# Expert layers of a one-core MoE kernel with weight chunks as the stationary operand, and scatter-adds ordered by expert

## What is computed

```
x = x + attention(layernorm(x))
t = rows of x                                  # 2048 tokens of 256
n = layernorm(t)
p = softmax(n @ router_w + router_b)           # 8 experts
top_v, top_i = top_k(p, 2); top_v /= sum(top_v)
for each expert e:
    h = silu(n @ gate_w[e] + gate_b[e]) * (n @ up_w[e] + up_b[e])     # 256 -> 512
    y[e] = h @ down_w[e] + down_b[e]                                  # 512 -> 256
t = t + sum of top_v * y[e] over the two chosen experts
```

## Time and profile before

| | |
|---|---|
| median of 3 runs | 454.25 us |
| all runs | 455.29, 454.06, 454.25 us |
| span of the profiled execution (first to last instruction) | 453.7 us |
| own time of the profiled execution | not given beside the span |
| busy, share of the span | PE 76%, DVE 76%, POOL 64%, ACT 46% |
| mean granted TensorE clock | 0.851 |

### The profile page before, as it was taken

How to read it: one execution, slowest core, us unless ns; L and a number is a source line. 1 busy time by engine, 2 the same in 40 slices (tenths; PEclk the granted TensorE clock), 3 DMA queues, 4 the chain that set the end, 5 groups by cost and what they waited for, 6 DMA issues and landing times.

```text
span 453.7 us, 13159 instructions
## 1 busy us (share of the span) xinstructions
PE 346.5 (76%) x4491; PEld 214.4 (47%) x4492; DVE 343.3 (76%) x693; ACT 209.2 (46%) x343; POOL 288.8 (64%) x459
## 2 busy tenths in 40 slices
PE   0078677767866766697259998999999999999971
PEld 0077434444444454542023654656566566565540
DVE  6988799799899999877882776666776776677650
ACT  1047637755956857645501433334434434433430
POOL 5616456666666666644585367777877878788651
PEclk9997568668668668689569999999999999999995
DMA  8410002322322222507764132333233333323322
GB/s 197 123 36 1 2 2 96 95 94 97 95 92 92 92 95 94 144 2 194 219 248 139 25 48 46 48 56 58 46 56 55 51 49 55 58 46 58 56 25 23
DMA packets 24960, 35.27 MB, mean 78 GB/s; under 512 B 4992, under 2 KB 18304, under 8 KB 24160
## 3 DMA queue, kind: packets, MB, share of 16 engines
q1 hardware_dynamic: 16256, 24.46, 17.5%
q0 software_dynamic: 7488, 10.23, 14.1%
q10 hardware_dynamic: 1184, 0.14, 0.2%
HBM read 25.39 MB, written 9.44 MB: 77 GB/s over the span
## 4 chain that ended last, share of the span: by engine, by line
PE 25%; DVE 23%; issue 19%; POOL 13%; DMA 9%; ACT 5%; DVEq 2%; POOLq 1%; SPq 1%; ACTq 0%
PE bank L881 6%; DMA w_stage<-token_rows,q_hi 5%; POOL w_stage L513 4%; PE bank L902 3%; POOL small L509 3%; DVE att L1348 2%; PE bank L549 2%; DVE s_exp L1314 2%; DVE v_exp L1367 2%; PE bank L777 2%; DVE q_exp L1382 2%; POOL v_exp L488 2%; PE bank L664 2%; DVE maxes L1307 2%; DMA token_rows<-z_stack 1%
## 5 line engine op out<-in xcount | busy, mean ns | idle before, releaser
L881 PE MATMUL bank<-w_exp,w_stage 128*128 x468 | 113.7, 380 | 1.3 <-issue 0.2
L526 POOL DMA_INDIRECT out_dram<-w_stage,q_hi x39 | 62.4, 1600 | 16.9 <-issue 16.9
L881 PEld LDWEIGHTS bank<-w_exp,w_stage 128*128 128x128 f16 x468 | 45.6, 97 | 41.8 <-issue 4.6
L408 POOL TENSOR_TENSOR w_exp<-w_stage,w_exp 128x1024 f16<-128x1024 f32 (+1 forms) x24 | 51.0, 2129 | 22.4 <-ACT w_exp L1041 22.4
L902 PE MATMUL bank<-w_exp,q_exp 128*128 x468 | 58.6, 276 | 2.1 <-DVE q_exp L1587 2.1
L513 POOL DMA_INDIRECT w_stage<-token_rows,q_hi x39 | 48.1, 1234 | 6.0 <-issue 6.0
L1570 DVE TENSOR_TENSOR v_exp<-bank,x_rows 128x512 f32<-128x512 f32 x39 | 27.0, 692 | 32.9 <-PE bank L881 32.8
L1146 ACT ACTIVATE w_stage<-w_stage,gate 128x256 f32<-128x256 f32 x39 | 19.8, 508 | 68.2 <-DVE w_stage L1592 68.2
L902 PEld LDWEIGHTS bank<-w_exp,q_exp 128*128 128x128 f16 x468 | 43.0, 98 | 11.8 <-issue 5.4
L1127 ACT ACTIVATE w_stage<-bank 128x256 f16<-128x256 f32 x39 | 14.9, 383 | 52.9 <-PE bank L869 52.9
L1587 DVE TENSOR_TENSOR q_exp<-bank,q_exp 128x512 f16<-128x512 f32 x39 | 27.0, 692 | 10.2 <-ACT q_exp L1138 10.0
(11 more groups left out here) (253 smaller groups left out, 814.2 us busy)
## 6 DMA issues: line engine op xcount, KB each, us to landing
w_stage<-in_L_ffn_gate_w_dram SPq DMA_DIRECT2D x8, 512.0 KB, 3.5
w_stage<-in_L_ffn_up_w_dram SPq DMA_DIRECT2D x8, 512.0 KB, 3.5
w_stage<-in_L_ffn_down_w_dram SPq DMA_DIRECT2D x8, 512.0 KB, 3.5
x_rows<-in_x_dram SPq DMA_DIRECT2D x8, 256.0 KB, 6.1
out_dram<-x_rows SPq DMA_DIRECT2D x4, 512.0 KB, 6.0
token_rows<-z_stack SPq DMA_DIRECT2D x4, 512.0 KB, 6.0
x_rows<-in_L_ffn_gate_b_dram SPq DMA_DIRECT2D x1, 2048.0 KB, 11.6
z_stack<-in_L_ffn_up_b_dram SPq DMA_DIRECT2D x2, 1024.0 KB, 6.8
```

The costliest lines, as they stand in the source:

```text
L408: pool.tensor_tensor(lo, w_stage[:, k, :], hi, ALU.subtract).then_inc(s["w_lo_done"], 1)
L526: pool.indirect_dma_start(out, bass.IndirectOffsetOnAxis(s_idx[par], 0), yw[par], None, compute_op=ALU.add).then_inc(s["y_scattered"], 16)
L881: mm = pe.matmul(GU[par][k][:], xs[par][:, c, :], w_exp[:, w * W_EXP + k * W_PIECE + c * FF:][:, bass.ds(e, FF)], start=(n == 0), stop=(n ...
```

## The change

In the expert stage:

- `hidden` swaps the operands: a chunk of 128 x 128 weights is stationary and the 128 tokens move. For each of 4 chunks of the 512 hidden columns, 2 halves of the inputs and 3 products there is one matmul of 128 columns, 24 for gate and 24 for up. The result has the hidden columns on the partitions, so `hidden_turned` goes.
- The gate and up biases are then one column each per chunk. They are loaded in the prologue as 64 rows of 128, transposed by PE, and kept in `b_cols`; SP's broadcasts go. ACT applies the gate bias within silu, in four instructions of 128 columns; DVE adds the up bias and multiplies in one instruction, four of 128 columns. Bias and silu columns start at the register of the expert's number, which ACT now loads too.
- All hardware loops of the expert stage are written out, 39 blocks one after the other. POOL's copies and holds go; an indirect DMA takes its indices straight from the table.
- Gathers 0 to 2 come first, then gather b + 3, scatter b.
- A scatter-add counts its landing on one of two semaphores, for even and odd blocks. Scatter b (from b = 2) waits for as many landings on each as two new tables `t_landed` say: those of the blocks of experts with lower numbers, at least the first of each; for empty blocks, those of all earlier blocks. `weigh(b)` waits for the landing of scatter b - 2, whose rows it overwrites.
- The order on DVE and ACT changes (at the diff's end).

```diff
+        b_cols = sb("b_cols", [P, 2 * EXPERTS * FF // P])
+        t_landed = [ga_flat[:, 256 + 64 * i:256 + 64 * i + BLOCKS].bitcast(i32) for i in range(2)]
...
+            for i, b in enumerate((gate_b, up_b)):
+                rows = slice(EXPERTS * FF // P * i, EXPERTS * FF // P * (i + 1))
+                sp.dma_start(b_rows[rows, :], b.rearrange("e (f p) -> (e f) p", p=P)).then_inc(s["r_in"], 16)
...
-            sp.dma_start(gate_b_all, gate_b.rearrange("e i -> (e i)").partition_broadcast(P)).then_inc(s["bias_rows"], 16)
...
-                sp.dma_start(up_b_all[:, half], up_rows[half].partition_broadcast(P)).then_inc(s["up_rows"], 16)
...
+            def gather(b):
+                if b >= 2:
                     pool.wait_ge(s["xt_ps"], b - 1)
+                pool.indirect_dma_start(xg[b % 2], None, token_rows,
+                                        bass.IndirectOffsetOnAxis(t_gather[:, b:b + 1], 0))\
+                    .then_inc(s[f"x_got{b % 2}"], 16)
+            def scatter(b):
+                landed = [pool.value_load(t_landed[i][0:1, b:b + 1], min_val=16, max_val=8 * BLOCKS + 8)
+                          for i in range(2)] if b >= 2 else []
                 pool.wait_ge(s["y_ready"], b + 1)
+                if b == 1:
+                    pool.wait_ge(s["y_landed0"], 16)
+                for i in range(len(landed)):
+                    pool.wait_ge(s[f"y_landed{i}"], landed[i])
+                pool.indirect_dma_start(out, bass.IndirectOffsetOnAxis(t_scatter[:, b:b + 1], 0), yw[b % 2], None,
+                                        compute_op=ALU.add).then_inc(s[f"y_landed{b % 2}"], 16)
+            for b in range(3):
+                gather(b)
+            for b in range(BLOCKS):
+                if b + 3 < BLOCKS:
+                    gather(b + 3)
+                if b == 0:
+                    pool.wait_ge(s["landed_ready"], 2)
+                scatter(b)
...
+                pe.transpose(bank[7][:, 256:256 + 2 * EXPERTS * FF // P], b_rows, ident[0:64, 0:64])
...
-                for xs, w in ((x_hi, 0), (x_hi, 1), (x_lo, 0)):
+                for f in range(FF_CHUNKS):
                     for c in range(2):
-                        mm = pe.matmul(GU[par][k][:], xs[par][:, c, :],
-                                       w_exp[:, w * W_EXP + k * W_PIECE + c * FF:][:, bass.ds(e, FF)],
-                                       start=(n == 0), stop=(n == 5))
+                        for xs, w in ((x_hi, 0), (x_lo, 0), (x_hi, 1)):
+                            mm = pe.matmul(GU[b % 2][k][:, P * f:P * f + P],
+                                           w_exp[:, w * W_EXP + k * W_PIECE + c * FF + P * f:][:, bass.ds(e, P)],
+                                           xs[b % 2][:, c, :], start=(c == 0 and xs is x_hi and w == 0),
+                                           stop=(c == 1 and w == 1))
...
-            def hidden_turned(b, par, first=False):
...
+            for b in range(BLOCKS):
+                if b + 1 < BLOCKS:
+                    e = weights_of(b + 1)
+                    hidden(b + 1, 0, e)
+                    hidden(b + 1, 1, e)
+                e = weights_of(b)
+                if b + 2 < BLOCKS:
+                    load_expert(b + 2)
+                    tokens_in(b + 2)
+                down(b, e)
...
+            def silu(b):
+                e = act.value_load(t_expert[0:1, b:b + 1], min_val=0, max_val=EXPERTS - 1)
+                if b >= 2:
+                    act.wait_ge(s["h_ready"], FF_CHUNKS * (b - 1))
+                act.wait_ge(s["gate_ps"], b + 1)
+                for f in range(FF_CHUNKS):
+                    act.activation(g_silu[b % 2][:, P * f:P * f + P], bank[2 * (b % 2)][:, P * f:P * f + P], ACT.Silu,
+                                   bias=b_cols[:, bass.ds(e * FF_CHUNKS + f, 1)]).then_inc(s["silu_ready"], 1)
...
+            for b in range(BLOCKS):
+                if b >= 1:
+                    weigh(b - 1)
+                if b + 1 < BLOCKS:
+                    silu(b + 1)
+                if b + 2 < BLOCKS:
+                    tokens_high(b + 2)
+                if b + 1 < BLOCKS:
+                    hidden_high(b + 1)
...
+            step(dve.tensor_tensor(r_ecmp, r_ecmp, r_nb.unsqueeze(1).broadcast_to([P, BLOCKS, EXPERTS]), ALU.mult))
+            step(dve.tensor_reduce(before_e, r_ecmp, AX.X, ALU.add))
+            step(dve.tensor_scalar(past, iota_f[:, 0:BLOCKS], r_cum[:, EXPERTS - 1:EXPERTS], 0.0, ALU.subtract, ALU.max))
+            for i in range(2):
+                step(dve.scalar_tensor_tensor(out=ints, in0=before_e, scalar=1.0 - i, in1=past,
+                                              op0=ALU.add, op1=ALU.add))
+                step(dve.tensor_scalar(ints, ints, 1, None, ALU.logical_shift_right))
+                step(dve.tensor_copy(halves[i], ints))
+                dve.tensor_scalar(t_landed[i], halves[i], 16.0, 16.0, ALU.mult, ALU.max).then_inc(s["landed_ready"], 1)
...
+            def gated(b):
+                e = expert_of(b)
...
+                dve.wait_ge(s["up_ps"], b + 1)
+                for f in range(FF_CHUNKS):
+                    cols = slice(P * f, P * f + P)
+                    dve.wait_ge(s["silu_ready"], FF_CHUNKS * b + f + 1)
+                    dve.scalar_tensor_tensor(
+                        out=h_sb[b % 2][:, cols], in0=bank[2 * (b % 2) + 1][:, cols],
+                        scalar=b_cols[:, bass.ds(e * FF_CHUNKS + EXPERTS * FF_CHUNKS + f, 1)],
+                        in1=g_silu[b % 2][:, cols], op0=ALU.add, op1=ALU.mult).then_inc(s["h_ready"], 1)
...
+            for b in range(BLOCKS):
+                if b >= 1:
+                    down_bias(b - 1)
+                if b + 1 < BLOCKS:
+                    gated(b + 1)
+                if b + 2 < BLOCKS:
+                    tokens_low(b + 2)
+                if b + 1 < BLOCKS:
+                    hidden_low(b + 1)
+            down_bias(BLOCKS - 1)
```

More of the change, by code:

```diff
@@ L529, in _ @@
-            gather(0, 0, first=True)
-            gather(0, 1, first=True)
-            gather(1, 0)
-            gather(1, 1)
-            scatter(0, 0, first=True)
-            with pool.Fori(0, 2 * BODY - 1) as i:
-                gather(i + 2, 0)
-                scatter(2 * i + 1, 1)
-                gather(i + 2, 1)
-                scatter(2 * i + 2, 0)
-            gather(2 * BODY + 1, 0)
-            for b in range(4 * BODY - 1, BLOCKS):
-                scatter(b, b % 2)
+                pool.indirect_dma_start(xg[b % 2], None, token_rows,
+                                        bass.IndirectOffsetOnAxis(t_gather[:, b:b + 1], 0))\
+                    .then_inc(s[f"x_got{b % 2}"], 16)
@@ L896, in down @@
+            def down(b, e):
                 pe.wait_ge(s["hl_ready"], b + 1)
-                if not first:
+                if b >= 1:
                     pe.wait_ge(s["yadd_ready"], b)
                 n = 0
-                for c in range(4):
+                for c in range(FF_CHUNKS):
                     for hs, w in ((h_hi, 0), (h_lo, 0), (h_hi, 1)):
-                        mm = pe.matmul(YB[:, 0:L_COL], hs[par][:, c, :],
+                        mm = pe.matmul(YB[:, 0:L_COL], hs[b % 2][:, c, :],
@@ L1161, in _ @@
-            with act.Fori(0, BODY) as i:
-                for k in range(4):
-                    act_block(4 * i + k + 1, (k + 1) % 2)
-            act_block(BLOCKS - 2, 1, more=1)
-            act_block(BLOCKS - 1, 0, more=0)
+            tokens_high(0)
+            silu(0)
+            tokens_high(1)
+            hidden_high(0)
+            for b in range(BLOCKS):
+                if b >= 1:
+                    weigh(b - 1)
[5 more added lines that the diff above has]
+                    hidden_high(b + 1)
@@ L1168, in _ @@
+            weigh(BLOCKS - 1)
         @block.vector
@@ L1555, in _ @@
             dve.wait_ge(s["tables_ready"], 1)
-            def tokens_low(b, par, first=False):
+            before_e, past = r_tab[:, 40:40 + BLOCKS], r_tab[:, 80:80 + BLOCKS]
+            halves, ints = [r_tab[:, 168 + 40 * i:168 + 40 * i + BLOCKS] for i in range(2)], r_ints[:, 128:128 + BLOCKS]
+            step(dve.tensor_tensor(r_ecmp, r_ecmp, r_nb.unsqueeze(1).broadcast_to([P, BLOCKS, EXPERTS]), ALU.mult))
+            step(dve.tensor_reduce(before_e, r_ecmp, AX.X, ALU.add))
+            step(dve.tensor_scalar(past, iota_f[:, 0:BLOCKS], r_cum[:, EXPERTS - 1:EXPERTS], 0.0, ALU.subtract, ALU.max))
@@ L1608, in _ @@
-            tokens_low(0, 0)
-            tokens_low(1, 1)
-            e0 = expert_of(0)
-            dve.wait_ge(s["bias_rows"], 32)
-            gate_bias(0, 0, e0, first=True)
-            dve.wait_ge(s["up_rows"], 32)
-            up_bias(0, 0, e0)
-            gated(0, 0, first=True)
-            dve_block(0, 0, first=True)
-            with dve.Fori(0, BODY) as i:
-                for k in range(4):
-                    dve_block(4 * i + k + 1, (k + 1) % 2)
-            dve_block(BLOCKS - 2, 1, more=1)
@@ L1621, in _ @@
```

(10 more changed lines are left out.)

210 lines of the change are left out of this document (56 added, 154 removed).

## The result

The changed kernel takes **507.03 us** (median of 4 runs, 506.11 to 507.31) against 454.22 us before (4 runs, 454.06 to 455.29): ratio 1.1165, 95% interval 1.1134 to 1.1196, slower. The profiled execution took 506.11 us, its span is 504.3 us, the mean granted clock 0.866. The prediction said 507 us.

What follows compares the result with a forecast made beforehand. PE and the scatter-add chain bound the old kernel; PE's sequencer and the DVE loop the new. 37 x (6.35 - 5.00) = +50.0, start +3.5, prologue +0.2, tail -0.5: +53 us, giving 507 us, range 478 to 545.

Steps and rivals of the forecast that it cites:

- PE's sequencer: On PE, 0.13 us per new register-addressed weight slice, 40 a block, 5.2 us; with the rest 6.2 to 6.3 us.
- PE's new work: Gate and up on PE become 48 matmuls of 128 columns, 55 ns each by the array, 2.64 us a block.
- The loop through DVE: From hidden's first slice through DVE's gated and tokens low back to PE: 6.39 us a block.
- the leg that I called just covered: PE's transposes, expert load and down, with gaps, expected to fit in the 2.2 us beside DVE's part.
- The period: Time from one down projection to the next: 6.35 us a block, against 5.00 before, over 37 periods.
- The start: First down projection expected 3.5 us later, as the first two blocks run at the new pace; prologue adds 0.2.
- The tail: After the thirty-eighth down, the last scatter-adds and POOL's drain: 0.5 us less than before.
- The other engines: ACT, DVE and POOL all stay below 6.35 us a block and cost nothing; freed scatter-adds gain nothing.
- Rival (A): Register operations hidden on PE, matmuls 55 ns apart, DVE loop 4.95 us a block: 452.6 us; chance 0.11.
- Rival (B): PE's clock falls below 0.9 as its work becomes short matmuls with gaps between them; chance 0.10.
- Rival (C): Gathers and scatter-adds stay the bound: 4.9 us a block, 452 us, only together with Rival (A); chance 0.02.

Runs made afterwards that it cites:

- more_ops: Changed kernel with the low-part tokens' weight slices shifted 64 columns, so hidden needs 48 register operations a block instead of 32: 587.54 us.
- early_tokens: Changed kernel with block b + 2's token transposes between gate and up on PE, and tokens low ahead of gated on DVE: 505.13 us.
- fixed_hidden: Changed kernel with gate and up weight slices at fixed addresses (expert 0's), so no register operations there: 454.97 us.
- short_loop: fixed_down with token transposes before the expert load, only one of gated's four instructions from block 2, and one wait for all silu slices: 483.41 us.
- serial: Changed kernel with every scatter-add again waiting for all earlier landings, constants replacing the two tables: 507.20 us.
- fixed_gate: Changed kernel with only gate's weight slices at fixed addresses (expert 0's), 24 register operations a block instead of 40: 453.47 us.
- fixed_down: Changed kernel with the slices of down's result at fixed addresses, 32 address operations a block instead of 40: 505.85 us.
- fixed_early: Changed kernel with the edits of both fixed_hidden and early_tokens: 506.93 us.
- moving_looped: Kernel before with POOL's new program and ACT's loop written out, but PE's and DVE's hardware loops kept: 447.46 us.

## Why the prediction was right, step by step

- **PE's sequencer.** The price of 0.13 us for an operation held: 0.13 in the changed kernel (4.1 / 31), 0.129 by the difference to more_ops, and 52 us vanish with the 32 operations of gate and up. The sum of 6.2 to 6.3 us was 6.23 in early_tokens, and by the sequencer's records it is this sum that sets the changed kernel's 6.27, with 0.04 us of waiting for DVE in it.
- **PE's new work.** 55 ns for a matmul with a fixed address ((0.61 - 0.22) / 7 is 55.7) was 56 in fixed_hidden.
- **The loop through DVE.** Forecast 6.39 us, measured 338.53 - 332.28 = 6.25 us in the block shown. Four terms differ. The product takes 4.28 us, not 4.03 + 0.14 + 0.22 = 4.39. DVE starts 0.34 us after the product's end (336.56 to 336.90), not 0.13. DVE's four instructions take 1.13 us, not 1.34 (estimated 0.29 each with gaps; they overlap), and tokens low starts 1.04 us after the first of them (337.94), not 1.40. From tokens low's end to gate it is 338.53 - 338.36 = 0.17 us, not 0.05. And the leg that I called just covered, load, tokens in and tokens high, ends at 337.80, 0.14 us before tokens low: it and gated are one wait in practice, which is why short_loop cuts both.
- **The period**: 6.35 taken, 6.27 measured; 37 x 0.08 = 3 us too many. **The start**: +3.7 with the prologue, measured +3.3, 0.4 us too many. **The tail**: -0.5 taken, +0.3 measured, so 0.8 us too few. The profiled execution stands 1.8 us above its span and the median 0.9 us above that, where I had carried over 0.55 us, 2.2 too few. The small errors nearly cancel; the exact 507 is luck within a range of a few microseconds.
- **The other engines.** POOL's two register loads (estimate 1.2 us) are two of 290 ns with 152 and 18 ns behind each, 0.92 us. ACT and DVE are busy 98.6 and 95.2 of 232 us. There is no wait for a gather or a landing in the 37 periods; the freed scatter-adds gained nothing, as serial shows.
- **Rival (A)** came true as soon as its condition was made: 4.95 us and 454.97 us with fixed addresses, though by a mixture of waits (4.76 us in the block shown). Its claim that the operations hide is true for the 24 a block of fixed_gate (gate and up in 2.85 us), false for 40 (4.28 us), and false for the 32 of fixed_down (4.23 us), where all of them stand behind the wait for tokens low.
- **Rival (B)**: the clock stayed at 1.00 through the 232 us. The forecast's upper end, 545 us, takes in part of (B), and no run shows a falling clock that makes the blocks that long: the lowest over the expert blocks of any run was 0.95 (fixed_early, 260 to 480 us, 6.34 us a block). **Rival (C)** did not appear with the change's own order. Its sign, PE waiting for a gather, appears once PE is faster, as (C) says (8 blocks of fixed_hidden), and with another order on DVE (7 blocks of early_tokens, 29 of fixed_early), there in a chain that (C) did not name, at 6.34 us a block and not 4.9.
- **What the prediction undervalued**: POOL's part with the written-out loops is worth 9 us by itself. In the changed kernel it is spent under a slower PE. With the matmuls of before the whole would be 444.77 us; the swapped operands, with their biases and the new orders, cost 507.0 - 444.8 = 62 us.

## What to carry to other kernels

A change that cuts long matmuls into short ones must be costed on the sequencer too: count the distinct register-computed addresses a block, times 0.13 us here, and compare the sum with the array's time since the sequencer's last wait. Below it the operations were free here (fixed_gate, 2.1 us of them under a product of 2.85), above it each further one was paid in full (more_ops, 0.129 us each). When two chains are equally long, taking away one of them can show next to nothing (here 1.9 or 1.2 us of 507, and 23.6 with both), so a null result needs the run that shortens both, or a look at whether the sequencer still stands at its wait. And a change with several parts should be timed by part: here one part is worth -9 us and another +62.

## What was not expected of the hardware

- The address operations on PE's sequencer come 0.13 us apart both with one matmul between two of them (more_ops, 48 in 336.7 to 342.8 us) and with one and two by turns (the changed kernel, 32 in 332.1 to 336.2 us), though the record of one operation is 46 ns long in both.
- Sixteen operations behind 24 matmuls without any did not lengthen the product: 2.85 us in fixed_gate and in fixed_hidden. The first of them came at 334.12 us, 0.36 us after the first of the 24 matmuls (333.76). In fixed_down the sequencer came to the wait for tokens low at 337.2 us and made its next operation for gate at 338.5, 1.3 us later.
- With fixed addresses, 48 pairs of weight load and 128-column matmul took 2.85 us, 56 ns a pair, at a granted clock of 1.00 (fixed_hidden, from 330.5 to 333.4 us).
- With the hardware loops of PE and DVE back (moving_looped), the block at the loop's turn takes 0.29 us more, every fourth one, where PE is the bound (5.02 against 4.73 us).
